# Fused Perceiver layer on one core: queries projected transposed, scores in two 64-row array tiles, TensorE order of the second half changed

## What is computed

```
x = x + fake_quant(layernorm(x)) @ fake_quant(ctx)             # ctx: one 1024x1024 matrix per batch
h = layernorm(x)
qkv = h @ Wqkv                                                 # 1024 -> 32 heads * 32 (q), 32 (k), 32 (v)
scores = einsum('bqhd,bkd->bhqk', q, k) * 32**-0.5             # one k and one v for all heads
scores = where(k <= q, scores + slope[h] * (k - q), -1e30)
x = x + (softmax(scores) @ v) @ Wo
y = layernorm(x)
r = softmax(y @ gate.T)                                        # 8 experts
x = x + (y * (r @ in_scale)) @ sign(weight).T * (r @ out_scale) + bias
```

## Time and profile before

| | |
|---|---|
| median of 3 runs | 470.25 us (469.28 to 470.58) |
| the profiled execution | 469.74 us |
| its span, first to last instruction | 467.7 us |
| TensorE busy, matmuls | 394.5 us (84%), 2720 |
| VectorE, ScalarE, GpSimd busy | 313.3, 281.1, 123.4 us |
| mean granted TensorE clock | 0.941 of full speed |
| chain that ended last, by engine | PE 69%, DVE 10%, ACT 8%, DMA 5%, issue 4% |

### The profile page before, as it was taken

One profiled execution on the slowest core, in us unless ns is written; L12 is line 12 of the kernel. 1 busy time (PEld: TensorE's weight loads), 2 busy tenths in 40 slices (PEclk: granted clock), 3 DMA queues, 4 the chain that ended last, 5 costly groups with the idle time before them and its releaser, 6 DMA issues.

```text
span 467.7 us, 7627 instructions
## 1 busy us (share of the span) xinstructions
PE 394.5 (84%) x2720; PEld 222.5 (48%) x2720; DVE 313.3 (67%) x596; ACT 281.1 (60%) x348; POOL 123.4 (26%) x148
## 2 busy tenths in 40 slices
PE   0433966779789999999999999999999999989565
PEld 0101434436445565556555655465556555645342
DVE  4308637888568759876987687769876885394331
ACT  2775588848795676567656774776487641351110
POOL 5201085235021322132222322231214121111202
PEclk9965887899999999999999999999999999999859
DMA  5995989678965854385438544754482001001001
GB/s 208 422 356 201 394 320 379 252 289 329 352 247 217 318 179 175 137 302 187 185 140 290 183 171 170 272 184 178 149 300 92 1 6 42 0 2 45 0 1 45
DMA packets 16968, 90.27 MB, mean 193 GB/s; under 512 B 3296, under 2 KB 3296, under 8 KB 8736
## 3 DMA queue, kind: packets, MB, share of 16 engines
q1 hardware_dynamic: 13408, 81.01, 46.8%
q10 hardware_dynamic: 3520, 8.69, 5.0%
HBM read 85.49 MB, written 4.19 MB: 192 GB/s over the span
## 4 chain that ended last, share of the span: by engine, by line
PE 69%; DVE 10%; ACT 8%; DMA 5%; issue 4%; POOL 2%; ACTq 1%; POOLq 0%; SPq 0%; DVEq 0%
PE R L1120 13%; PE R L1121 12%; PE R L1122 12%; PE R L1318 11%; PE T L1165 10%; ACT b L487 5%; PE C L1146 4%; PE T L1277 3%; DMA ring<-ctx 2%; DMA ring<-L_attn_Wqkv 2%; DVE Wo_lo L759 1%; DMA quant<-L_xattn_x_zp 1%; PE T L1296 1%; PE R L1310 1%; DVE st L797 1%
## 5 line engine op out<-in xcount | busy, mean ns | idle before, releaser
L487 ACT ACTIVATE b<-ring,quant,qpar 128x2048 uint8<-128x2048 f32 x64 | 132.9, 2092 | 11.2 <-DMA ring<-ctx 8.7
L1120 PE MATMUL R<-Wo_hi,attT_hi 128*128 128x512 f16 x128 | 48.6, 380 | 6.4 <-DVE Wo_lo L759 4.6
L1120 PE MATMUL R<-Wqkv_hi,T_hi 128*128 128x512 f16 x128 | 49.7, 388 | 0.0
L1318 PE MATMUL R<-sgn,T_hi 128*128 128x512 fp8e4 x128 | 49.7, 388 | 0.0
L1318 PE MATMUL R<-sgn,T_lo 128*128 128x512 fp8e4 x128 | 49.5, 387 | 0.0
L1121 PE MATMUL R<-Wqkv_lo,T_hi 128*128 128x512 f16 x128 | 49.5, 387 | 0.0
L1122 PE MATMUL R<-Wqkv_hi,T_lo 128*128 128x512 f16 x128 | 49.5, 387 | 0.0
L1121 PE MATMUL R<-Wo_lo,attT_hi 128*128 128x512 f16 x128 | 48.5, 379 | 0.0
L1122 PE MATMUL R<-Wo_hi,attT_lo 128*128 128x512 f16 x128 | 48.5, 379 | 0.0
L1146 PE MATMUL C<-b,aT 128*64 128x512 f16 x256 | 38.7, 430 | 10.3 <-ACT b L487 6.6
L413 POOL TENSOR_TENSOR small<-small,consts 128x1 f32<-128x1 f32 x24 | 7.4, 309 | 145.9 <-DVE small L804 145.9
(11 more groups left out here) (137 smaller groups left out, 886.4 us busy)
## 6 DMA issues: line engine op xcount, KB each, us to landing
ring<-ctx SPq DMA_DIRECT2D x64, 1024.0 KB, 4.8
ring<-L_attn_Wqkv SPq DMA_DIRECT2D x8, 544.0 KB, 5.7
XN<-x ACTq DMA_DIRECT2D x8, 512.0 KB, 4.5
ring<-L_attn_Wo SPq DMA_DIRECT2D x4, 1024.0 KB, 5.2
ring<-L_ffn_weight SPq DMA_DIRECT2D x4, 1024.0 KB, 5.0
out<-X ACTq DMA_DIRECT2D x8, 512.0 KB, 2.7
alibi_sb<-alibi SPq DMA_DIRECT2D x1, 512.0 KB, 6.7
bias_sb<-L_ffn_bias SPq DMA_DIRECT2D x1, 512.0 KB, 7.8
```

What stands on the lines that cost most here:

```text
L487: e.activation(b8[:, c % BRING, :], ring[:, slot, :], ACT.Identity, scale=qR2, bias=qZ2).then_inc(s_rf[slot], 1)
L1120: e.matmul(dst, lhs[0], rhs[0], start=first, stop=False)
L1318: last = e.matmul(R[:, 2 + n, :], T16[part][:, k, :], sgn[:, k, n * HALF:(n + 1) * HALF], start=k == 0 and part == 0, stop=k == KT - 1 and ...
```

## The change

What is computed and what is loaded of the context stay as they are. What changes:
- The projection makes q transposed. The weights are stationary (128 columns), T16 is moving (128 columns); a head group of four heads lands in R with channels on the partitions. 192 matmuls instead of 48. There is no `q_copy` and no `tq` for q; `q_hi` and `q_lo` read R2 and R3 directly. Only k is still copied and transposed (`tk`).
- `kbd` becomes a two-block matrix, 2 x 64 columns, in each 64-row half of the partitions; it is written whole, with a mask of ones and zeros (`pair_sb`, one more small DMA) as scale, in two instructions instead of four each on ScalarE and VectorE. Its zeroing by GpSimd goes.
- `scores(s, b)`: each matmul uses 64 rows of the array and 128 columns; the two halves of the rows alternate and write different banks. 48 matmuls. Both halves of a batch's heads come at once. The head order in the table and in the rows of Wo is changed on the host to suit.
- TensorE's order: all scores at the end of the second half; context(·, 2) at the start of the first half; query(1) spread over router and context. VectorE's and ScalarE's orders follow.

```diff
     T_ORDER = [("M", "PT00"), ("M", "PT01"), ("M", "PT10"), ("M", "PT11"), ("M", "Ta0"), ("M", "Ta1"),
                ("F", "T10"), ("F", "T11"), ("M", "T20"), ("M", "T21"), ("F", "Tk"), ("M", "rl"),
-               ("F", "Tq0"), ("N", "T0"), ("M", "rT"), ("F", "Tq1"), ("M", "is0"), ("M", "is1")]
+               ("N", "T0"), ("M", "rT"), ("M", "is0"), ("M", "is1")]
...
-        kbd = [sb(f"kbd_{p}", [P, 2, 4 * S], F16) for p in ("hi", "lo")]
+        kbd = [sb(f"kbd_{p}", [P, 2, 2 * S], F16) for p in ("hi", "lo")]
...
             def q_hi(s, c):
...
+                e.wait_ge(s_qT, s.i * 2 + c + 1)
+                if c == 0:
+                    at_least(e, s_sc, s.i * 2)
+                hi_part(qT[0][:, :, 4 * c:4 * c + 4, :].rearrange("p b g t -> p b (g t)"),
+                        R[:, 2 + c, :].rearrange("p (b q) -> p b q", b=2), dq, s_qhi)
+
+            def k_hi(s):
+
+                e.wait_ge(s_Tk, s.i + 1)
+                at_least(e, s_sc, s.i * 2)
+                for j in range(2):
+                    last = e.activation(kbd[0][:, :, j * S:(j + 1) * S],
+                                        T[:, s.bank("Tk"), 0:P].rearrange("p (b k) -> p b k", b=2),
+                                        ACT.Identity, scale=pair_sb[:, j:j + 1])
+                last.then_inc(s_khi, 1)
...
+            def query(s, n, ks=range(KT)):
+
                 if n == 0 and k_low(ks):
                     at_least(e, s_an, s.i * 4)
...
+                    rows = [t[:, k, :].rearrange("p (b t) -> p b t", b=2) for t in T16]
+                    for g in range(4):
+                        dst = R[:, 2 + n, :].rearrange("p (b g t) -> p g b t", b=2, t=S)[:, g]
+                        at = (4 * n + g) * P
+                        hi, lo = (w[:, k, at:at + P] for w in Wqkv)
+                        e.matmul(dst, hi, rows[0], start=k == 0 and g == 0, stop=False,
+                                 skip_group_check=True)
+                        e.matmul(dst, hi, rows[1], start=False, stop=False, skip_group_check=True)
+                        last = e.matmul(dst, lo, rows[0], start=False, stop=k == KT - 1,
+                                        skip_group_check=True)
...
+            def scores(s, b):
+
+
+                if b == 0:
                     emptied(s, "Tk")
-                    emptied(s, "Tq0")
+                    e.wait_ge(s_qlo, s.i * 2 + 2)
                     at_least(e, s_x2, s.i * 2)
...
+                for pair in range(4):
+                    for x, y in ((0, 0), (0, 1), (1, 0)):
+                        for r in range(2):
+                            rows = slice(64 * r, 64 * r + 64)
+                            lhs = qT[x][rows, b, 2 * pair:2 * pair + 2, :].rearrange("p g t -> p (g t)")
+                            last = e.matmul(R[:, 2 * b + r, pair * P:(pair + 1) * P], lhs,
+                                            kbd[y][rows, b, :], start=x + y == 0, stop=x == 1)
                 last.then_inc(s_sc, 1)
...
             def first_half(s):
                 f, m, b = s.front, s.middle, s.back
+                if f:
+                    context(s.i, 2)
                 if b:
                     outscale(s, 0)
...
                 if m:
                     ta(s, 0)
                     pv(s, 1, 0)
-                if f:
-                    context(s.i, 2)
-                if m:
                     pv(s, 1, 1)
...
+                if f and m:
+                    query(s, 1, high[:2])
                 if n:
                     context(s.i + 1, 0, s)
-                if f and not s.is_step(0):
-                    qkv(s, 1, high[2:])
-                if f:
-                    scores(s, 0, 0)
-                    scores(s, 0, 1)
                 if m:
                     router_t(s)
-                if f:
-                    tq(s, 1)
+                if f and m:
+                    query(s, 1, high[2:])
                 if m:
                     inscale(s, 0)
                 if n:
...
                 if m:
                     inscale(s, 1)
                 if f:
-                    scores(s, 1, 0)
-                    scores(s, 1, 1)
+                    scores(s, 0)
+                    scores(s, 1)
```

More of the change, by code:

```diff
@@ L1083, in second_half @@
                 if f:
[L1084 removed]
+                    scores_in(s.i, 0, 0)
+                if m:
+                    xs(s, 1)
+                if f:
+                    scores_in(s.i, 0, 1)
+                if m:
+                    xs_lo(s, 0)
+                if f:
                     row_max(s.i, 0, 0)
                 if m:
[L1087 to L1088 removed]
+                    xs_lo(s, 1)
                 if f:
                     subtract_max(e, s.i, 0, 0)
[L1091 to L1092 removed]
             run_steps(e, first_half, second_half, chain)
@@ L1172, in t1, with kv @@
                                s_T1)
-            def qkv(s, n, ks=range(KT)):
-                if n == 2 and k_low(ks):
+            def kv(s, ks=range(KT)):
+                if k_low(ks):
                     emptied(s, "T10")
@@ L1179, in qkv @@
                     e.wait_ge(s_x1, s.i + 1)
+                for k in ks:
+                    if s.is_step(0):
+                        e.wait_ge(s_rf[k % RING], 3 + k // RING)
+                    last = split_product(C[:, 0, 0:2 * D], [t[:, k, :] for t in T16],
+                                         [w[:, k, H:NQKV] for w in Wqkv], k == 0, k == KT - 1)
+                if ks[-1] == KT - 1:
+                    last.then_inc(s_kv, 1)
+            def query(s, n, ks=range(KT)):
                 if n == 0 and k_low(ks):
@@ L1192, in tq @@
-            def tq(s, c):
-                e.wait_ge(s_q, s.i * 3 + (c + 1) % 3 + 1)
-                if c < 2:
-                    transposes(s, f"Tq{c}",
-                               [q_sb[:, g * P:(g + 1) * P] for g in range(4 * c, 4 * c + 4)], s_Tq)
-                else:
-                    transposes(s, "Tk", [q_sb[:, H:H + P]], s_Tq)
-            def scores(s, h, b):
-                if h == 0 and b == 0:
+                    rows = [t[:, k, :].rearrange("p (b t) -> p b t", b=2) for t in T16]
@@ L1204, in scores, with tk @@
+                if ks[-1] == KT - 1:
+                    last.then_inc(s_qT, 1)
+            def tk(s):
+                e.wait_ge(s_k, s.i + 1)
+                transposes(s, "Tk", [k_sb[:, :]], s_Tk)
+            def scores(s, b):
+                if b == 0:
                     emptied(s, "Tk")
-                    emptied(s, "Tq0")
+                    e.wait_ge(s_qlo, s.i * 2 + 2)
                     at_least(e, s_x2, s.i * 2)
-                if h == 1 and b == 0:
-                    emptied(s, "Tq1")
@@ L1209, in scores @@
-                for half in range(2):
-                    pair = 2 * h + half
-                    lhs = [t[:, b, 2 * pair:2 * pair + 2, :].rearrange("p g t -> p (g t)") for t in qT]
-                    last = split_product(R[:, 2 * b + h, half * 256:(half + 1) * 256],
-                                         lhs, [k[:, b, :] for k in kbd], True, True)
+                for pair in range(4):
[5 more added lines that the diff above has]
+                                            kbd[y][rows, b, :], start=x + y == 0, stop=x == 1)
```

151 lines of the change are left out of this document (62 added, 89 removed).

## The result

| | before | after |
|---|---|---|
| median | 470.41 us (469.28 to 471.55, 4 runs) | 476.37 us (475.03 to 479.53, 4 runs) |
| ratio after to before | | 1.0136, 95% interval 1.0078 to 1.0194 |
| the profiled execution, its span | 469.74, 467.7 us | 479.53, 477.7 us |

The change makes the kernel slower by 1.4%. Forecast was 469.3, no change, with 465.3 to 475.5 as range; the measured time lies outside it. The profiled execution is the longest of the four; the gap between the two profiled spans is 10.0 us, that between the medians 6.0.

A forecast was written before the change was run, and what follows sets the result against it. TensorE was taken to bound the steady step (46.69 of 47.20 us). Terms 0.4 + 1.1 + 3.0 + 0.35 - 5.85 = -1.0 gave 468.7 profiled, a median of 469.3 us, no change, range 465.3 to 475.5.

The forecast's parts named there:

- Five hand-overs: Step changes into steps 3 to 7: the projection starts 1.17 us earlier in each, -5.85 us in all.
- my layout's own: Whole kernel as the prediction laid it out: 469.3 us, own range 467.8 to 470.8, chance 0.42.
- Query 55.7 ns a matmul, +0.34: Query projection in a steady step: 192 matmuls of 128 columns take 10.70 us instead of 10.36.
- R3: Rival, slower: a 128-column matmul costs 69 ns, 2.55 us a step more, 490 us; chance 0.04.
- R4: Rival, slower: weight load only half hidden, 78 ns a matmul, 4.3 us a step more, 504 us; chance 0.02.
- Score pairs together: Scores in a steady step: 48 matmuls in 64-row tiles run two at a time, 1.34 us, -1.3 us.
- R2: Rival, slower: 64-row score pairs do not overlap, hand-over gain 0.5 instead of 1.17, 474.6 us; chance 0.13.
- Moving context(i, 2), no change: First half of a step: moving this product to its start changes where 0.99 us is paid, not how much.
- Late next: Hand-over between steps: TensorE waits for VectorE, 0.9 us before outscale(0) and 0.35 before outscale(1); net -1.17 us a step.
- R5: Rival, faster: TensorE's whole 2.35 us a step comes through, another 5.9 us less, 463.4 us; chance 0.04.
- Start-up +4.5: Kernel's start: constants +0.4, step 0 to 1 +1.1, step 1 to 2 +3.0 with TensorE idle 5.5 us.
- Tile 7 and the tail +0.35: Step 7 to 8: TensorE waits for VectorE with no context product to fill, +0.35 us; tail from 430 us unchanged.

The follow-up runs named there:

- e1: Changed kernel with its eight steps written out one behind the other, no loop and so no jump back: 470.88 us.
- e5: Changed kernel with 64 waits on a long-up semaphore ahead of TensorE's first work, moving the loop's head by 32 instructions: 470.61 us.
- e3: Changed kernel with context(2,2) moved back to the middle of the first half, in step 2 alone: 469.87 us.
- e11: e5 (loop kept, head moved by 32 instructions) with context(2,2) of step 2 back in the middle of the first half: 466.02 us.
- e10: As e8, but each block's score matmuls run as twelve of the upper 64 rows, then twelve of the lower, not in turn: 470.29 us.
- e9: As e8, but context(i, 2) stands in the middle of the first half in every step: 473.81 us.
- e2: Kernel before the change with its eight steps written out, no loop and no jump back: 469.33 us.
- e8: Changed kernel with steps written out and context(2,2) of step 2 back in the middle of the first half: 465.25 us.
- e4: Changed kernel with each context load in the loop's steps bringing 256 of 2,048 columns, the rest left out of the computation: 475.8 us.
- e7: Kernel before the change with 354 idle waits (177 instructions) ahead of TensorE's first work, to leave 100 instructions behind the jump: 485.18 us.
- e6: Kernel before the change with 372 idle waits (186 instructions) ahead of TensorE's first work, to leave 21 instructions behind the jump: 487.4 us.

## Why the prediction was wrong

**The step that failed is the sum's list of stretches**: "Five hand-overs (into steps 3 to 7) are of this kind: -5.85. DMA, GpSimd and SP keep their order and have room." The fourth of these hand-overs, into step 6, holds the loop's jump back, and the prediction had no term for it. In the trace of before the jump shows as 0.42 us of issue, and the prediction says nothing of it, which puts its change at nothing without a reason. But this price belongs to the place of the head in a packet of instructions, and a change that adds 954 instructions ahead of the loop (2,865 to 3,819) draws that place anew: 207 left became 21, or 191 became 5 as the traces count. The missing term is +9.3 in the profile and 5.5 to 5.8 in the medians (e1, e5; 3.9 between e3 and e11), of the 7.1 by which the forecast missed. Without it the changed kernel takes 470.9 (e1) or 470.6 (e5), inside the range and about the upper end of my layout's own (470.8); the rest is points 7 and 8 below.

Point by point:
1. *Query 55.7 ns a matmul, +0.34:* right. Timeline of the changed kernel, 96 of them:
```profile
254.59 0.22 PE L1204 MATMUL R<-T_hi,Wqkv_hi 128*128 128x128 f16 x1
...
259.95 1.04 PE L1171 MATMUL T<-ident,XL 128*128 128x128 f32 x8
```
5.36 / 96 = 55.8 ns, each with its own load. So R3 (69) and R4 (78) are out. The 81 that the Trainium skill gives for such a stream ("TensorE: Matmul & The Clock Gate", "Back-to-back issue gap") is not what this trace shows either.
2. *q transposes, -1.0, and 4., the wait of 0.40:* right; neither is in the timeline any more.
3. *Score pairs together:* right, 56 ns a pair; e10 shows that it comes from the order in turn, so R2's mechanism exists, and this code avoids it.
5. *Moving context(i, 2), no change:* right only with the hand-over beside it; e9 prices its place at 0.79 a step and more where the clock falls.
6. *Late next:* 0.9 before outscale(0) and a steady step of 46.03 were forecast. The changed kernel:
```profile
275.06 0.38 PE L1326 MATMUL R<-outsc,rT 32*128 32x512 f16 x1 [1.01 <-DVE T_lo L759]
...
277.38 0.39 PE L1326 MATMUL R<-outsc,rT 32*128 32x512 f16 x1
...
279.43 1.29 PE L1171 MATMUL T<-ident,Pr 128*128 128x128 f32 x8
```
1.01 before outscale(0). Outscale(1) starts 2.32 behind outscale(0) where it was 2.15 before, so its wait is 0.2 and not 0.35. R5 is out.
7. *Start-up +4.5:* 4.9, taken at the transposes of step 2 (158.26, before 153.32), but part of this nearness is luck. The first two terms, 0.4 and 1.1, come to 0.9 at the transposes of step 1 (102.47 for 101.57), and to -0.1 between e1 and e2, where the edits are the same. The third, 3.0, comes to 4.0 in both pairs. The wait was forecast as 5.5 and was 5.35; the half clock lasted through all of the first FFN half, 3.5 us where I took 2.5, which is about that 1.0. What I had not seen is that the same product in its old place makes this stretch 1.0 to 1.9 us shorter than in the kernel before (e11, e8, e3). The loss was avoidable, and worth 5.3 to 5.9 in this stretch.
8. *Tile 7 and the tail +0.35:* 0.8, which says little. From the sixth outscale to the end the changed kernel took 100.67 us, and e1, e3, e4, e5 and e7, with the same code there, 98.7 to 99.8; the kernel before took 99.88, e2 and e6 98.6 and 100.3. Between e1 and e2 it is +1.0.

The signs of the terms in a steady step were right and most sizes within 0.1 us. With the jump out of the picture the change gains 1.0 to 1.2 in a steady step and gives it back in the start-up and the tail: written out, 470.88 against 469.33, and in the spans of these two -4.9 in the hand-overs, +4.6 in the start-up and +1.0 behind.

## What to carry over

In this program the price of the loop's jump back, 0.6 to 10.0 us, went with the place of its head in the stream of instruction packets, and the same body could have either. When a change adds or takes instructions on an engine that is the bound, look for "issue" at the first instructions behind the jump, and try the loop written out or a few idle instructions ahead of it before judging the change itself. An order that is good in the steady step may be bad in one early step where data come late: there the old place, for that step alone, gave back 4.6 to 6.5 us of the median.

## What the runs showed of the hardware

- Around the jump one packet of 16,384 bytes lands, and the next one does not follow at once. From the landing of the first to the start of the second: 5.2 us in the changed kernel, 3.4 in e3, 3.7 in e6, 4.9 in e7; hidden behind work 3.5 in the kernel before, 3.6 in e5, 5.3 in e11; in all these the DMA engines were 0.7 busy or more. In e4, with them nearly idle, 2.7. From the landing of the packet that TensorE waits for to its next matmul it was 1.2 to 1.6 us in the changed kernel, e3, e4, e6 and e7.
- How long the stall is differs with the same code at the jump: 6.6 us in the changed kernel's profiled execution, the slowest of its four, and 4.4 in e3's. So the 10.0 us between the spans is more than the 6.0 between the medians, and the light loads of e4 shorten the stall in the trace (6.6 to 3.8) but not the median (475.8 for 476.37). Why stays open, and so does what sets the gap of 2.7 us when nothing else moves.
- A wait on a semaphore that is long up isn't free: 186 and 177 of these instructions delayed TensorE's first work to 31.67 and 30.70 us. Nine fewer are 0.97 us less, so about 0.11 us each, as an estimate from these two runs.
